# A decoder layer for 32 batches on one core: new instruction orders and lags for all queues, SyncE's transfers ordered as one serial queue, and separate variance columns

## What is computed

```python
x = x + self_attention(layernorm(x))      # with a bias by relative position
x = x + cross_attention(layernorm(x), ctx, ctx, mask)
x = x + ffn(layernorm(x))                 # 128 -> 512 (gate, up) -> 128, quantised

def self_attention(x):
    xn = layernorm(x) * ln_g + ln_b
    q, k, v = split(xn @ w_qkv + b_qkv)
    attn = softmax(q @ k.T * scale + rel_bias)
    return (attn @ v) @ w_out + b_out
# the feed-forward part: silu(bitlinear(x, w_gate)) * bitlinear(x, w_up), then bitlinear(., w_down);
# bitlinear rounds activations to 8 bits by row and weights to -1, 0, 1
```

## Time and profile before

| | value |
|---|---|
| median of 3 runs | 522.55 us |
| lowest and highest run | 516.62 and 526.21 us |
| profiled execution | 516.4 us |
| its span | 514.3 us |
| TensorE busy | 400.9 us (78%) |
| VectorE busy | 382.4 us (74%) |
| ScalarE busy | 348.0 us (68%) |
| GpSimd busy | 282.7 us (55%) |
| SP's queue, share of 16 engines' span | 46.9% |
| mean granted TensorE clock | 0.949 |

### The profile page before, as it was taken

One profiled execution on the slowest core, in us unless ns is written; L12 is line 12 of the kernel. 1 busy time (PEld: TensorE's weight loads), 2 busy tenths in 40 slices (PEclk: granted clock), 3 DMA queues, 4 the chain that ended last, 5 costly groups with the idle time before them and its releaser, 6 DMA issues. The chain is left out here.

```text
span 514.3 us, 18102 instructions
## 1 busy us (share of the span) xinstructions
PE 400.9 (78%) x5501; PEld 322.8 (63%) x5532; DVE 382.4 (74%) x1928; ACT 348.0 (68%) x962; POOL 282.7 (55%) x784
## 2 busy tenths in 40 slices
PE   2245786898897888799988878878889986877762
PEld 2234565677686777687776667767678765645431
DVE  5732856599697888789988878878869986886553
ACT  2113565688687888698887778877869875865442
POOL 5610565588465666666665666665637653563221
PEclk9999998899899999899999999999989998997785
DMA  5634565556445564556555455455556443324200
GB/s 171 182 108 111 130 156 136 156 136 155 131 123 142 151 163 129 146 156 162 143 153 140 123 146 163 127 142 137 151 148 169 133 128 108 87 71 134 67 7 10
DMA packets 100180, 67.27 MB, mean 131 GB/s; under 512 B 73269, under 2 KB 90421, under 8 KB 100085
## 3 DMA queue, kind: packets, MB, share of 16 engines
q1 hardware_dynamic: 98209, 64.08, 46.9%
q10 hardware_dynamic: 1876, 2.03, 1.2%
HBM read 46.08 MB, written 19.07 MB: 127 GB/s over the span
## 5 line engine op out<-in xcount | busy, mean ns | idle before, releaser
L943 DVE CUSTOM_DVE_ANT_0 biased<-bank,mask_bias 128x128 bf16<-128x128 f32 x512 | 115.2, 285 | 11.0 <-PE bank L1188 8.8
L948 DVE TENSOR_REDUCE neg_max_S<-bank 128x4 f32<-128x512 f32 x128 | 84.4, 681 | 28.2 <-PE bank L1188 27.9
L634 ACT ACTIVATE probs_S<-bank 128x512 f32<-128x512 f32 x128 | 71.9, 591 | 46.7 <-PE bank L1206 46.7
L634 ACT ACTIVATE probs_X<-bank 128x512 f32<-128x512 f32 x128 | 75.0, 587 | 21.5 <-PE bank L1206 21.3
L1206 PE MATMUL bank<-stack_q_S,stack_k_S 122*128 122x128 bf16 x512 | 50.1, 236 | 44.5 <-DMA stack_q_S<-neg_maxT_S 43.9
L442 POOL TENSOR_SCALAR veps_F<-mv_F 128x1 f32<-128x1 f32 x32 | 6.1, 192 | 119.0 <-DVE mv_F L846 119.0
L1206 PEld LDWEIGHTS bank<-stack_q_S,stack_k_S 122*128 122x128 bf16 x512 | 34.1, 106 | 56.7 <-issue 47.7
L1188 PE MATMUL bank<-stack_k_S,stack_q_S 120*128 120x128 bf16 x512 | 49.2, 233 | 17.2 <-DMA stack_q_S<-scratch_rel 12.7
L1188 PE MATMUL bank<-stack_k_X,stack_q_X 72*128 72x128 bf16 x512 | 51.3, 224 | 5.0 <-DMA stack_k_X<-scratch_X 4.8
L1203 PE MATMUL bank<-ident_bf,mask_bias 128*128 128x512 bf16 x128 | 50.7, 396 | 3.9 <-DMA stack_q_X<-neg_maxT_X 3.8
L1206 PEld LDWEIGHTS bank<-stack_q_X,stack_k_X 74*128 74x128 bf16 x512 | 41.0, 100 | 17.0 <-issue 2.5
(11 more groups left out here) (175 smaller groups left out, 1165.8 us busy)
## 6 DMA issues: line engine op xcount, KB each, us to landing
stack_q_S<-scratch_S SPq DMA_DIRECT2D x32, 288.0 KB
stack_k_S<-scratch_S SPq DMA_DIRECT2D x32, 288.0 KB
stack_q_X<-scratch_X SPq DMA_DIRECT2D x32, 288.0 KB
stack_k_X<-scratch_X SPq DMA_DIRECT2D x32, 288.0 KB
scratch_S<-qk_parts_S SPq DMA_DIRECT2D x32, 192.0 KB, 4.1
scratch_X<-qk_parts_X SPq DMA_DIRECT2D x32, 192.0 KB, 3.7
ctxT<-ctx SPq DMA_DIRECT2D x8, 256.0 KB, 3.8
scratch_S<-qk_parts_S SPq DMA_DIRECT2D x32, 64.0 KB, 3.3
```

The source lines that it names most:

```text
L634: act.activation(probs[a][:, b % 2, c, :], bank_b[c % 2][:, :], ACT.Exp).then_inc(sems["exp_" + a], 1)
L943: last = dve.tensor_tensor_reduce(biased[:, c, hh, :], quarter(bank_a[c % 2], hh), mask_bias[:, b % 2, :], -1.0, -2.0 * BIG, ALU.add, ALU.min,
L948: dve.tensor_reduce(neg_max[a][:, first_head(c):first_head(c) + 2 * HC - 1:2], bank_a[c % 2][:, :].rearrange("i (h j) -> i h j", h=HC), AX ...
```

## The change

Three edits. First, the lists `fill`, `step` and `drain` of all five engines are written anew, with other orders and lags, and `LEAD, TAIL` go from 2, 3 to 3, 4. Second, `veps_s` gets a column for every batch, and `var_group` no longer waits for the power of the group before. Third, `rel_split` on VectorE stands ahead of `fill` and no longer behind a group of LayerNorm statistics in it. No function that issues work is changed but for `var_group` and `pow_group`.

```diff
-LEAD, TAIL, LAGS = 2, 3, 12
+LEAD, TAIL, LAGS = 3, 4, 12
...
-        veps_s = sb("veps_S", [S, GROUP])
+        veps_s = sb("veps_S", [S, B])
...
             def fill(st):
-                stack_in("S", st, 0)
-                max_in("S", st, 1)
-                load_c(st, -2)
-                load_x(st, -2)
-                parts_again("S", st, -1)
-                parts_out("S", st, -1)
+                max_in("S", st, 2)
+                parts_again("S", st, 0)
+                parts_out("S", st, 0)
                 if st.at(0):
                     rel_rows(sp, stack_q)
                 if st.at(1):
                     rel_copies(sp)
+                load_c(st, 0)
+                load_x(st, -2)
+                stack_in("S", st, 0)
...
                     pool.wait_ge(sems["mv_S"], hi)
-                    if g:
-                        pool.wait_ge(sems["rstd_S"], g)
-                    pool.tensor_scalar(veps_s[:, 0:hi - lo], mv_s[:, lo:hi, 1], 1.0 + EPS, EPS * EPS, ALU.mult, ALU.add)\
+                    pool.tensor_scalar(veps_s[:, lo:hi], mv_s[:, lo:hi, 1], 1.0 + EPS, EPS * EPS, ALU.mult, ALU.add)\
...
             def fill(st):
-                attend_sums("S", st, 4)
-                ln_group(st, -2)
-                ternary_weights(st, 0)
-                if st.at(-1):
-                    rel_split()
...
+            rel_split()
             run(begun, fill, step, drain)
```

More of the change, by code:

```diff
@@ L538, in fill @@
             def fill(st):
-                pow_group(st, 4)
-                var_group(st, 11)
-                neg_group(st, 3)
                 var_group(st, -1)
+                pow_group(st, -1)
+                rest("S", st, 0)
                 part3("S", st, 0)
@@ L545, in fill @@
                     clear_values("X")
-                neg_group(st, -1)
+                max_hi("S", st, 2)
+                max_lo("S", st, 2)
+                neg_group(st, 2)
+                var_group(st, 3)
                 pow_group(st, -1)
+                neg_group(st, -2)
                 normalise_s(st, -1)
-                max_hi("S", st, 1)
-                max_lo("S", st, 1)
-                rest("S", st, -1)
             def step(st):
+                var_group(st, -2)
+                max_hi("S", st, 2)
@@ L554, in step @@
+                normalise("F", st, 5)
+                max_lo("S", st, 2)
+                part3("X", st, 2)
+                gate_unit(st, 5)
+                quantise_y(st, 5)
+                rest("S", st, 0)
+                inverse_std("X", st, 1)
                 part3("S", st, 0)
-                mask_to_bias(st, 3)
-                neg_group(st, 1)
                 normalise_s(st, -1)
-                variance("F", st, 5)
-                negate_mean("F", st, 5)
-                rest("X", st, 2)
@@ L575, in step @@
                 normalise("X", st, 1)
+                mask_to_bias(st, 2)
+                neg_group(st, -1)
                 max_hi("X", st, 3)
                 max_lo("X", st, 3)
+                variance("X", st, 0)
+                negate_mean("X", st, 0)
+                rest("X", st, 1)
+                variance("F", st, 4)
+                negate_mean("F", st, 4)
+                inverse_std("F", st, 4)
+                pow_group(st, -2)
             def drain(st):
+                rest("X", st, 44)
@@ L580, in drain @@
+                inverse_std("F", st, 6)
                 normalise("F", st, 6)
+                normalise("X", st, 1)
+                inverse_std("X", st, 0)
+                part3("X", st, -15)
+                variance("X", st, -7)
+                gate_unit(st, 6)
                 quantise_y(st, 6)
-                gate_unit(st, 6)
+                h_units(st, 6)
                 mask_to_bias(st, 3)
-                rest("X", st, 1)
                 max_hi("X", st, 4)
-                variance("X", st, 7)
@@ new lines, in fill @@
+                exp("S", st, 2, 3)
+            def step(st):
+                part2("X", st, 2)
+                o_raw_out("S", st, 3)
+                exp("X", st, 4, 0)
+                qk_out("S", 0, st, 0)
+                qk_out("S", 1, st, 0)
+                part1("S", st, 0)
+                maxT_out("S", st, 2)
+                exp("X", st, 4, 1)
+                v_out("S", st, 0)
+                oT_out("S", st, 3)
+                part2("S", st, 0)
+                yT_out(st, 5)
+                exp("X", st, 4, 2)
+                exp("X", st, 4, 3)
+                tanh(st, 5)
+                o_raw_out("X", st, 4)
+                exp("S", st, 2, 0)
+                xnT_out("X", st, 1)
+                exp("S", st, 2, 1)
+                maxT_out("X", st, 3)
+                exp("S", st, 2, 2)
+                qk_out("X", 0, st, 1)
+                exp("S", st, 2, 3)
+                qk_out("X", 1, st, 1)
+                oT_out("X", st, 4)
+                quantise_h(st, 5)
+                part1("X", st, 1)
+                hT_out(st, 5)
+                v_out("X", st, 1)
+                xnT_out("S", st, -1)
@@ L1108, in drain @@
                 row_max("X", st, 3, 0)
+                y_max(st, 5)
                 out_scaling(st, 6)
-                ln_moments("X", st, -10)
-                y_max(st, 5)
                 y_unit(st, 5)
```

294 lines of the change are left out of this document (125 added, 169 removed).

## The result

The changed kernel takes 476.64 us (median of 4 runs, 474.74 to 481.47), the kernel before beside it 521.11 (516.62 to 526.21). The medians lie 44.5 us apart. The forecast was 492 in a range of 476 to 515, 30 us off.

What follows compares the result with a forecast made beforehand. The prediction took SP's queue, a 12.1 us loop of one pair after the other, as the bound. Steps 20.9 + ramp 2 + start 7 = 30 us off 522.55 gave 492 us, range 476 to 515.

Steps and rivals of the forecast that it cites:

- SP's loop of two landings: SP's queue before: each pair of stacks waits for parts landing behind the other pair, 6.1 + 6.0 = 12.1 us a step.
- the forecast's own first case: Change works as planned: step 11.7 to 12.7, start gains 5 to 9, 477 to 503 us; chance 0.60.
- the extra 256 KB: SP's queue: about one further ctx, mask, x or out transfer a step delays X's pair, 0.3 us above 12.0.
- One landing a step instead of two: SP's queue after: only X's parts, issued behind S's pair, are still waited for before X's next pair.
- cover and need are level: TensorE, S's maxima: 3.7 us of cover against 3.6 needed, so most of the 1.46 us wait a step goes.
- the bound of 11.7: Lower bound of the step: TensorE's 11.2 us plus 0.5 for one late pair.
- the forecast's loop of 11.0: SP's new loop between X pairs: 9.9 us plus 1.1 for 256 KB, below TensorE's 11.2 a step.
- The same loop at less load: The five steps ahead of the steady window, where X fills up: 2 us gained.
- Depth, tail and columns: Pipeline depth with one more `LEAD`, the stretch behind 420.9 us, and `veps_s` columns: each costed at 0 us.
- The second: SP blocks at S's `part3` ahead of X's pair, so gain stays small: 512 us, or 517; chance 0.24.
- The third: Loop through S's maxima on TensorE and SP lengthens, step 14.2, 538 us; chance 0.13.
- The fourth: One step more in the pipeline and no gain in the steps: 530 us; chance 0.03.

Runs made afterwards that it cites:

- the run with the start freed: Changed kernel with clearing of X's value tile on GpSimd moved behind batch 2's normalising and VectorE's feed-forward weight sums one fill call earlier: 476.28 us, 0.917.
- SP's place undone: Changed kernel with only the two writes of S's parts put back behind X's pair and X's maxima in SP's step: 517.99 us, 1.001 of the kernel before.
- SP's order alone: Kernel before with only both writes of S's parts moved ahead of X's pair in SP's step, engines' lists unchanged: 530.58 us, 1.026 of the kernel before.

## Why the prediction was right, and where its sizes were off

**What bound the kernel: right.** The step of 12.1 to 13.25 was SP's loop of two landings. Putting back one of SP's places puts back 41 us with every other list new; more DMA costs the kernel before 1.36 us a step, and more TensorE work nothing.

**The range: hit by luck.** The result is 0.6 us inside its low end, and just outside the 477 to 503 us of the forecast's own first case. The working is 11.5 us short of the span's gain: 6.7 in the steps, 3.5 ahead of them, 1.3 behind.

**The step, 12.3 forecast, 11.99 measured.** The failed term is the 0.3 put on top of 12.0 for the extra 256 KB ahead of X's pair, with the 0.3 to 0.8 of new wait for X's stacks that was meant to show it. TensorE's wait for X's stacks is 1.0 us in 22 steps. Two steps of the working were wrong with it. "One landing a step instead of two" should have been none: the forecast took X's parts as still issued right behind S's pair, while they are now ready later and go out 3.2 and 5.2 us behind the first half of it, where they land in a median of 2.6 us. And "cover and need are level" for S's maxima: the 8 KB now leave SP 0.4 us behind the start of ScalarE's copy (205.8 to 206.19) and with no pair ahead of them still in flight, so the wait is 0 and not 0.3 a step. The 16 DMA engines are 0.86 busy from 204 to 205 us and 0.32 from 205 to 206.

**The floor came out right, its reason did not.** The forecast took 12.0 from one quiet step of the trace before as the nearest row for a step with little waiting; 22 steps now take 11.99 each, and that agreement is in part luck. TensorE's work was taken as 11.2, from that one step, though the mean of the earlier trace rows is 11.5; it measures 11.69 now. So the bound of 11.7, built as 11.2 and 0.5 for a late pair, is in truth TensorE's work alone, and the forecast's loop of 11.0 lies 0.7 below it, not 0.2. By the runs with more and less TensorE work a second limit of about 11.9, which the forecast did not have, lies on top.

**The start and the ramp, 7 + 2 forecast, 12.5 measured.** The bias rows went out at 16.64 (forecast 15 to 18). "The stacks of batch 0 land at about 25" failed: in the run with the start freed they land at about 28.5, for a pair issued at the same time. The likely reason, not shown, is that ctx, whose first load I took as gone from ahead of them, stands with x right ahead of the pair. So the first scores gain 2.8 us and not 5. The second batch's scores start at 37.11, where it was 43.30: 6.2 sooner, in the 5 to 9 forecast and near the 7 taken. The rest, 12.5 - 6.2 = 6.3 us, is the ramp, forecast as 2. "The same loop at less load" under-sized it: with SP's place undone, the stacks of batch 9 start at 131.0, so the ramp's gain, and more, hangs on the same place in SP's list. The split is not a clean one: with the bias rows early in the old lists 7.7 us at batch 1 were 3.0 at batch 9, so the start's 6.2 need not have lasted, and the ramp may have gained more than 6.3.

**Depth, tail and columns: right at 0**, apart from 1.3 us behind the last S stacks. With four shared columns again no difference in time can be told.

**The rivals.** The second's mechanism, SP stopped at S's parts ahead of X's pair, took 3.0 us a step for ScalarE's part and 0.8 for GpSimd's in the old lists (530.58 us), and 0.2 and 0.3 in the new. The forecast looked for it at GpSimd's `part3`; in the old lists it was mostly ScalarE's `part2` that SP stood for. The third did not come: the copy of the maxima is at 205.8 and the transfer's issue at 206.19, and no wait for it is left. The fourth would have shown behind the last S stacks, and did not.

**The signs named beforehand:** the landing wait for S's parts gone, yes (0.2 us); that for X's remaining, no (1.5); a gap of low DMA share once a step, yes in the step read (0.10 from 213 to 214 us, 0.32 or more in the rest from 202 us on); TensorE's wait for S's maxima down to 0.3 a step, it fell to 0; X's stacks 0.3 to 0.8 a step, no; stacks of S each 12.3 us, 11.99; first scores at 25, 27.97.

## What to carry to other kernels

In a queue that serves in order, a wait for a landing costs more when the write is issued right behind a large transfer: put the write ahead of it, or leave time between the write and whoever waits for it. Such an order is only as good as the engines' lists that feed it: much the same move in SP's list was worth 41 us with lists made for it, and cost 12 us without. When one limit is removed, count the next ones: here two lay within 0.3 us of each other in the steady state, and two at the same time at the start, so easing one of them alone brought a fifth of what was eased, or nothing that could be told. And a start's gain must be followed to the steady steps before it is booked: 7.7 us at batch 1 were 3.0 at batch 9.

## What the runs showed of the hardware

The same writes of X's parts, 64 and 192 KB, land in a median of 3.9 us behind a pair of stacks and of 2.6 us with a gap ahead. 384 KB a step added to the queue cost 0.93 us in one kernel and 1.36 in the other, where the bytes at the stacks' rate would take 1.7. The Trainium skill, DMA: Bandwidth & Descriptors, section Anatomy of one DMA, fits a DMA of GpSimd's path as 2.0 us and the bytes at 436 GB/s, by which the bytes alone of the same 384 KB are an estimated 0.9 us. These writes go by SP's queue, for which no run has that fit; the kernel before, where the queue binds, shows more than the 0.9.

The granted clock from 150 to 350 us was 0.98 in the kernel before, 0.94 with SP's order alone and 1.00 in the changed kernel, where 1.00 is the 2.4 GHz level and 1.2 GHz the other. The waits of TensorE's matmuls do not explain it by their length: with the bias rows early the clock there was 1.00, with 25.4 us of waits for S's maxima in 15 times, and in the kernel before 0.98, with 22.2 us in 14.
